# Causal scores of a step in three tiles of probabilities instead of four

## What is computed

```python
q_lat = jnp.einsum('bhsd,hdr->bhsr', q_nope, wuk)
scores = jnp.einsum('bhsr,btr->bhst', q_lat, c_kv) + jnp.einsum('bhsd,btd->bhst', q_rope, k_rope[:, 0])
causal = jnp.tril(jnp.ones((s, s), dtype=bool))
scores = jnp.where(causal, scores, jnp.finfo(scores.dtype).min)
probs = jax.nn.softmax(scores, axis=-1)
out_lat = jnp.einsum('bhst,btr->bhsr', probs, c_kv)
```

## Time and profile before

| | |
|---|---|
| median of 3 runs | 1919.72 us (1919.02 to 1920.83) |
| span of the profiled execution | 1917.3 us |
| instructions | 32648 |
| granted TensorE clock in the attention | 1.00 |

### The profile page before, as it was taken

One profiled execution on the slowest core, in us unless ns is written; L12 is line 12 of the kernel. 1 busy time (PEld: TensorE's weight loads), 2 busy tenths in 40 slices (PEclk: granted clock), 3 DMA queues, 4 the chain that ended last, 5 costly groups with the idle time before them and its releaser, 6 DMA issues.

```text
span 1917.3 us, 32648 instructions
## 1 busy us (share of the span) xinstructions
PE 1909.2 (100%) x10048; PEld 1615.0 (84%) x10048; DVE 1531.8 (80%) x2655; ACT 1168.9 (61%) x2648; POOL 1048.7 (55%) x891
## 2 busy tenths in 40 slices
PE   9999999999999999999999999999999999999999
PEld 7888888888888888888888888888888877888887
DVE  6778888888888887877777777777878889996677
ACT  5456767676758575765555555555656668766441
POOL 5468777787869696865555556555565511000000
PEclk9999999999999999999999999999999999999999
DMA  9838474647474655588546264464628286466645
GB/s 361 333 105 317 133 260 130 253 125 263 122 266 138 231 171 199 195 319 328 181 151 233 77 230 132 158 207 140 217 82 302 91 285 250 198 220 245 229 152 176
DMA packets 86473, 393.13 MB, mean 205 GB/s; under 512 B 9472, under 2 KB 10240, under 8 KB 67328
## 3 DMA queue, kind: packets, MB, share of 16 engines
q1 hardware_dynamic: 86400, 392.21, 58.0%
HBM read 236.46 MB, written 155.71 MB: 205 GB/s over the span
## 4 chain that ended last, share of the span: by engine, by line
PE 97%; DVE 2%; DMA 1%; ACT 0%; issue 0%; DVEq 0%; POOL 0%; ACTq 0%; SPq 0%
PE at_out L1281 11%; PE at_out L1285 10%; PE at_out L1282 10%; PE at_qbank L55 7%; PE at_qbank L57 7%; PE at_qbank L56 7%; PE at_score L1244 6%; PE at_score L1235 3%; PE at_turned L1256 3%; PE at_qbank L1605 3%; PE at_score L1605 2%; PE at_out L1605 2%; PE at_value L56 2%; PE at_value L55 2%; PE at_value L57 2%; PE at_qbank L1608 2%
## 5 line engine op out<-in xcount | busy, mean ns | idle before, releaser
L2620 DVE TENSOR_TENSOR at_acc<-at_out,at_acc 128x512 f32<-128x512 f32 x640 | 438.9, 689 | 138.2 <-PE at_out L1285 136.2
L2266 POOL TENSOR_TENSOR at_acc<-at_stage,at_acc 128x512 f32<-128x512 f32 x256 | 332.3, 1298 | 184.1 <-ACT at_stage L1747 174.5
L1281 PE MATMUL at_out<-at_wvo,at_val_hi 128*128 128x512 f32 x896 | 365.3, 408 | 0.5 <-ACT at_stage L1747 0.2
L1285 PE MATMUL at_out<-at_wvo,at_val_lo 128*128 128x512 f32 x896 | 350.6, 391 | 0.0
L1282 PE MATMUL at_out<-at_wvo,at_val_hi 128*128 128x512 f32 x896 | 350.5, 391 | 0.0
L1747 ACT ACTIVATE at_stage<-at_out 128x512 f32<-128x512 f32 x256 | 153.0, 599 | 125.2 <-PE at_out L1285 112.9
L1787 ACT ACTIVATE at_pT_hi<-at_turned 128x512 fp32r<-128x512 f32 x128 | 76.4, 597 | 245.8 <-PE at_turned L1256 245.8
L2226 POOL TENSOR_TENSOR at_probs<-at_probs,at_row_stats 128x512 f32<-128x512 f32 x128 | 133.3, 1041 | 148.2 <-DVE at_row_stats L2582 148.2
L1781 ACT ACTIVATE at_probs<-at_probs,at_row_stats 128x128 f32<-128x128 f32 x512 | 197.7, 388 | 8.8 <-DVE at_row_stats L2577 8.8
L1285 PEld LDWEIGHTS at_out<-at_wvo,at_val_lo 128*128 128x128 f32 x896 | 168.4, 188 | 37.8
L1281 PEld LDWEIGHTS at_out<-at_wvo,at_val_hi 128*128 128x128 f32 x896 | 169.1, 189 | 31.1 <-DVE at_acc L2620 5.7
(11 more groups left out here) (313 smaller groups left out, 4772.3 us busy)
## 6 DMA issues: line engine op xcount, KB each, us to landing
parts_d<-at_rope_tmp SPq DMA_DIRECT2D x32, 1024.0 KB, 6.1
at_qrope<-parts_d SPq DMA_DIRECT2D x128, 256.0 KB, 5.3
wvo_d<-at_wvo SPq DMA_DIRECT2D x16, 2048.0 KB, 7.8
at_wvo<-wvo_d SPq DMA_DIRECT2D x16, 2048.0 KB, 8.1
ff_w_d<-ff_w SPq DMA_DIRECT2D x21, 1024.0 KB, 6.2
ff_w<-ff_w_d SPq DMA_DIRECT2D x21, 1024.0 KB, 4.8
ab_raw<-in_w_heads SPq DMA_DIRECT2D x32, 576.0 KB, 5.5
wvo_d<-at_wvo SPq DMA_DIRECT2D x16, 1024.0 KB, 9.8
```

The lines of the kernel that those rows point to most:

```text
L1281: pe.matmul(out, hi, weight[:, 0], start=start, stop=False, skip_group_check=True)
L1285: pe.matmul(out, lo, weight[:, 0], start=False, stop=True, skip_group_check=True).then_inc(out_ready, 1)
L2266: pool.tensor_tensor(at, stage[group][z][:], at, ALU.add).then_inc(pool_added, 1)
L2620: dve.tensor_tensor(at, outb[FACTORS[name][2]][:], at, ALU.add).then_inc(added, 1)
```

## The change

The four score tiles of a step become three. Late queries (64 to 127) of both heads of a batch share the rows of one tile with all 128 keys, one tile for each batch. Early queries (0 to 63) of both heads have only keys 0 to 63; both batches stand side by side in the columns of the third tile. For this the queries are stored by half (`half_of`: late or early) with both heads in 128 adjacent columns, so ScalarE writes at_qlat in pieces of 64 and the relayout of the rotated queries writes runs of 64 tokens: 16 DMAs of [32, 8, 64] for four, and the semaphore's counts go from 64 to 256. The turned probabilities are taken out in three pieces on ScalarE and VectorE; their lower left quarter is cleared once, in the opening. The mask covers late keys' half and the early tile. The blocks of values change places, with their homes in memory; the matmuls of values and products keep their sizes.

```diff
@@ relayout_in
                 for j in range(4):
-                    sp.dma_start(as_f32(qrope[c][j * HALF:(j + 1) * HALF]), of[SLOT_OF_PART[j]]).then_inc(
-                        qrope_in[c], 16)
+                    for h in range(QUAD):
+                        to = as_f32(qrope[c][j * HALF:(j + 1) * HALF, h // PAIR, :, h % PAIR])
+                        sp.dma_start(to, of[SLOT_OF_PART[j]][:, h].rearrange("p (k q) -> p k q", q=HQ)).then_inc(
+                            qrope_in[c], 16)
@@ TensorE score_ropes
                 for bl in range(2):
-                    cols = batch_cols(s, bl)
-                    for h in range(PAIR):
-                        pe.matmul(score[:, bl * PAIR + h], qrope[c][:, pair * PAIR + h, cols], rope_keys[:, :, cols],
-                                  start=h == 0, stop=False, skip_group_check=True)
+                    pe.matmul(score[:, bl], both_heads(qrope[c][:, pair, half_of(s, bl, 1)]), rope_keys[:, :, batch_cols(s, bl)],
+                              start=bl == 0, stop=False, skip_group_check=True)
+                for bl in range(2):
+                    pe.matmul(score[:, EARLY, :, early_keys(bl)], both_heads(qrope[c][:, pair, half_of(s, bl, 0)]),
+                              rope_keys[:, :, early_cols(s, bl)], start=bl == 0, stop=False, skip_group_check=True)
@@ TensorE score_rests
                 for bl in range(2):
-                    cols = batch_cols(s, bl)
-                    for h in range(PAIR):
-                        ins = pe.matmul(score[:, bl * PAIR + h, 0], qlat[u % 2][:, h, cols], compressed[c][:, cols],
-                                        start=False, stop=True, skip_group_check=True)
+                    pe.matmul(score[:, bl, 0], both_heads(qlat[u % 2][:, half_of(s, bl, 1)]), compressed[c][:, batch_cols(s, bl)],
+                              start=False, stop=True, skip_group_check=True)
+                for bl in range(2):
+                    ins = pe.matmul(score[:, EARLY, 0, early_keys(bl)], both_heads(qlat[u % 2][:, half_of(s, bl, 0)]),
+                                    compressed[c][:, early_cols(s, bl)], start=False, stop=True, skip_group_check=True)
@@ TensorE turn
-                for j in range(PARTS):
-                    to = TURNED_AT[j]
-                    ins = pe.transpose(turned[:, to * SEQ:(to + 1) * SEQ], probs[s % 2][:, j, :], ident[:])
+                for to, tile in enumerate((1, 0, EARLY)):
+                    ins = pe.transpose(turned[:, to * SEQ:(to + 1) * SEQ], probs[s % 2][:, tile, :], ident[:])
@@ ScalarE
-                act.activation(qlat[u % 2][:, h, :], qbank[use % 2][:], ACT.Copy).then_inc(ql_out, 1)
+                act.activation(qlat[u % 2][:, :, h, :], qbank[use % 2][:].rearrange("p (k q) -> p k q", q=HQ),
+                               ACT.Copy).then_inc(ql_out, 1)
...
-                    ins = act.activation(probs[i][:, j, :], probs[i][:, j, :], ACT.Exp,
-                                         bias=nmax[i][:, j:j + 1], accum_out=sums[i][:, j:j + 1])
+                    rows = probs[i][:, j, :] if j < EARLY else probs[i][:, EARLY, early_keys(j - EARLY)]
+                    ins = act.activation(rows, rows, ACT.Exp, bias=nmax[i][:, j:j + 1], accum_out=sums[i][:, j:j + 1])
...
-                act.activation(pT_hi[:], turned[:], ACT.Copy).then_inc(pT_hi_done, 1)
+                act.activation(pT_hi[:, :, HQ:SEQ], late_turned, ACT.Copy).then_inc(pT_hi_done, 1)
+                for bl in range(2):
+                    act.activation(pT_hi[0:HQ, heads_at(bl), 0:HQ], early_turned[bl], ACT.Copy).then_inc(pT_hi_done, 1)
@@ GpSimd normalise
-                pool.tensor_tensor(probs[i][:], probs[i][:], rsum[i].unsqueeze(2).to_broadcast([P, PARTS, SEQ]),
+                late, early = probs[i][:, LATE], probs[i][:, EARLY].rearrange("p (b k) -> p b k", b=2)
+                pool.tensor_tensor(late, late, rsum[i][:, 0:2].unsqueeze(2).to_broadcast([P, 2, SEQ]), ALU.mult)
+                pool.tensor_tensor(early, early, rsum[i][:, 2:4].unsqueeze(2).to_broadcast([P, 2, HQ]),
                                    ALU.mult).then_inc(probs_ready, 1)
@@ VectorE turn
-                dve.wait_ge(pT_hi_done, STEPS * m + s + 1)
-                dve.tensor_tensor(pT_lo[:], turned[:], as_f32(pT_hi[:]), ALU.subtract).then_inc(pT_lo_done, 1)
+                done = 3 * (STEPS * m + s)
+
+                def early(bl):
+                    to = slice(0, HQ), heads_at(bl), slice(0, HQ)
+                    return dve.tensor_tensor(pT_lo[to], early_turned[bl], as_f32(pT_hi[to]), ALU.subtract)
+
+                dve.wait_ge(pT_hi_done, done + 2)
+                early(0)
+                dve.wait_ge(pT_hi_done, done + 3)
+                dve.tensor_tensor(pT_lo[:, :, HQ:SEQ], late_turned, as_f32(pT_hi[:, :, HQ:SEQ]), ALU.subtract)
+                early(1).then_inc(pT_lo_done, 1)
```

More of the change, by code:

```diff
@@ L136, in decoder, with high @@
     PRODUCTS, PLAIN = 7, 3
[L137 to L142, removed]
+    BLOCKS = PRODUCTS + 1
+    A21, A22, A11, A12, S2, S3, S4, S1 = (slice(j * SEQ, (j + 1) * SEQ) for j in range(BLOCKS))
+    DIRECT, SUMS = slice(SEQ, 4 * SEQ), slice(4 * SEQ, BLOCKS * SEQ)
+    A11_A12, S3_S4 = slice(A11.start, A12.stop), slice(S3.start, S4.stop)
+    HQ, HALVES = SEQ // 2, 2 * BPC
+    LATE, EARLY = slice(0, 2), 2
+    TILES = 3
+    def high(of):
+        return slice(of.start - SEQ, of.stop - SEQ)
     FACTORS = {"P1": (A11, "b11", 0), "P2": (A12, "b21", 1), "P6": (S2, "t2", 0), "P5": (S1, "t1", 0),
@@ L219, in decoder @@
         probs = [home(157696 + 2048 * i, f"at_probs{i}", [P, PARTS, SEQ]) for i in range(2)]
[L220 to L225, removed]
+        pT_both = home(161792, "at_pT", [P, 2, 2 * PAIR, SEQ], F32R)
+        pT_hi, pT_lo = pT_both[:, 0], pT_both[:, 1]
+        val_hi = [home(o, f"at_val_hi{i}", [P, PRODUCTS * SEQ], F32R) for i, o in enumerate((75776, -6144))]
+        val_lo = [home(o, f"at_val_lo{i}", [P, BLOCKS * SEQ], F32R) for i, o in enumerate((79360, 88064))]
+        val_whole = [home(o, f"at_val_whole{i}", [P, BLOCKS * SEQ]) for i, o in enumerate((79360, 88064))]
         stage_at = (4 * (PACK + UNUSED), 4 * UNUSED, 198656)
@@ L316, in decoder @@
         prep_turned = outb[1]
+        late_turned = turned[:, 0:2 * SEQ].rearrange("p (k q) -> p k q", q=HQ)
+        early_turned = [turned[bl * HQ:(bl + 1) * HQ, 2 * SEQ:3 * SEQ].rearrange("p (k q) -> p k q", q=HQ) for bl in range(2)]
         cr_turned, cr_out = qbank, [turned, value]
@@ L396, in batch_cols, with early_cols, half_of, both_heads @@
             return slice(b * SEQ, (b + 1) * SEQ)
+        def early_cols(s, bl):
+            return slice(batch_cols(s, bl).start, batch_cols(s, bl).start + HQ)
+        def half_of(s, bl, late):
+            return 2 * (2 * (s % 2) + bl) + late
+        def both_heads(of):
+            return of.rearrange("p h q -> p (h q)")
+        def early_keys(bl):
+            return slice(bl * HQ, (bl + 1) * HQ)
+        def heads_at(bl):
+            return slice(PAIR, 2 * PAIR) if bl == 0 else slice(0, PAIR)
         def place(s):
@@ L1268, in values @@
                     cols = batch_cols(s, bl)
-                    at = slice(bl * PAIR * SEQ, (bl + 1) * PAIR * SEQ)
-                    ins = three_passes(pe, value[:, at], tok[:, c, KV_HI + cols.start:KV_HI + cols.stop],
+                    at = heads_at(bl)
+                    ins = three_passes(pe, value[:, at.start * SEQ:at.stop * SEQ], tok[:, c, KV_HI + cols.start:KV_HI + cols.stop],
                                        tok[:, c, KV_LO + cols.start:KV_LO + cols.stop],
@@ L1278, in product @@
                 val, op, n = FACTORS[name]
-                out, hi, lo, weight = outb[n][:], val_hi[s % 2][:, val], val_lo[s % 2][:, val], wvo[pair][op]
+                out, hi, lo, weight = outb[n][:], val_hi[s % 2][:, high(val)], val_lo[s % 2][:, val], wvo[pair][op]
                 pe.matmul(out, hi, weight[:, 0], start=start, stop=False, skip_group_check=True)
@@ L2675, in opening @@
                 largest(0, 0)
+                dve.memset(as_f32(pT_both[HQ:P, :, :, 0:HQ]), 0.0)
                 query(N - 1, 1)
@@ L3090, in constants @@
         "ident": np.eye(P, dtype=np.float32),
-        "mask": np.where(np.tril(np.ones((SEQ, SEQ), bool)), 0, MASKED).astype(np.float32),
+        "mask": np.concatenate([np.zeros((P, SEQ // 2)), np.tile(np.where(np.tril(np.ones((SEQ // 2, SEQ // 2), bool)), 0, MASKED),
+                                                                  (2, 1))], axis=1).astype(np.float32),
         "cos": np.tile(cos * root, (QUAD, 1)),
```

42 lines of the change are left out of this document (24 added, 18 removed).

## The result

The changed kernel takes 1945.4 us (median of four runs, 1943.2 to 1947.3), the kernel before 1920.3 on the same chip: a ratio of 1.0129, interval 1.0115 to 1.0144. It is 25 us slower, where 12 us faster was forecast.

The account below looks back on a forecast made before the run. TensorE's matmul stream, 97% of the chain, was taken to bound the kernel: 0.128 us less in each of 128 steps gains 16.4 us, losses 4.4, so 1919.7 - 12.0 gives 1908 us; range 1900 to 1932.

Parts of the forecast that it names:

- What it adds elsewhere: Added work on VectorE, ScalarE and GpSimd, mostly covered; waits in slots 0 and 1, opening and last quad lose 4.4 us.
- The relayout: cost 0, without any cover left: SyncE's 16 issues take 7.6 us for 1.89; raw rope weights queued behind land at 707.9, just not late; cost 0.
- Rival C: Short 256-byte runs make the relayout late, and the raw rope load behind it; 1942 us, or 1925 for half; chance 0.17.
- D: TensorE's f32r matmuls with 128 moving columns are slow, priced as fp32, 0.22 us a step for 0.11; 1936 us; chance 0.06.
- E: Side engines' small strided pieces grow the turn's chain by over 0.66 us, so values wait each step; 1920 us; chance 0.12.
- B: Narrow TensorE matmuls cost what their columns stream, saving another 0.30 us a step; 1874 us; chance 0.10.
- floor: On TensorE a narrower moving operand still costs 0.110 us (f32r, 128 columns) and 0.10 us an fp32 instruction.
- rests: The score block's fp32 matmuls on TensorE: eight instructions before and after, half of them narrow; 0 us gained by the floor.
- the wait for the turn: Slot 0 of group 0's quads: values wait 0.10 to 0.26 us for VectorE's turn, taken as 0.18, in seven quads, 1.3 us.
- opening and last quad: Chains with cover under 0.3 us in three or four slots, and one clearing of turned probabilities; 1.0 us lost.
- the bound of 0.29: VectorE's turn in three pieces for one subtraction grows by at most 0.29 us, taken as 0.21.
- the cover of a plain slot: VectorE's turn ends with 0.66 us to spare before the values' weight load, so its and ScalarE's growth costs nothing there.

Follow-up runs that it names:

- the shifted kernel: The changed kernel with 24 empty VectorE instructions near its start, so its loop over the full quads begins 24 instructions later; 1920.4 us, ratio 1.000 to the kernel before.
- the shift of a loop of the same length: The kernel before with five empty VectorE instructions in each slot of the full loop (297 instructions) and 40 more near the start; 1960.5 us, ratio 1.021.
- the written-out loop: VectorE's six full-quad iterations written out, in the unshifted changed kernel with halves put side by side on the relayout's store: 1906.6 us; in the kernel before: 1920.9 us.
- experiment 5: The changed kernel with 4 empty VectorE instructions near its start; 1956.1 us, ratio 1.019.
- experiment 1: The changed kernel with 24 empty VectorE instructions near its start; 1920.4 us, ratio 1.000 to the kernel before.
- experiment 7: The changed kernel with 24 empty VectorE instructions and the relayout's halves put side by side on the store (256-byte runs), loaded back by 4 DMAs; 1907.4 us, ratio 0.994.
- the cured kernel: The changed kernel with 24 empty VectorE instructions and the relayout's halves put side by side on the store to memory, the kernel of experiment 7; 1907.4 us.

## Why the prediction was wrong

**The step that failed first is one that I did not take**: of the sum over engines, no term asked whether the longer programs still stay on the engines. "What it adds elsewhere" counted VectorE's added instructions by their time, some of them hidden, and never by their number. Forty more in the full loop, placed as they are, cost 4.6 to 6.4 us in slot 0 of five quads, 25.0 us in the end against the shifted kernel. The runs show the cause in three ways: the shift by 24 takes it away, the shift of a loop of the same length brings it into the kernel before, and the written-out loop has none. Not shown is how many stretches stay on VectorE; three, with 257 or 297 instructions, do, and one position more does not. That the boundaries are those of the 8 KB packets is inferred, and the traces bear it out. In the changed kernel a third wait, of 0.4 us, stands ahead of the loop's instruction 136 (five of the six in the row L2668 of the list of waits), 128 instructions behind the second one, and in the quad from 416 us the last two packets of q14 start at 475.89 and 519.93 us, 0.7 and 2.7 us behind the loop's instructions 136 and 264. The Trainium skill, "Vector Engine (DVE) Microarchitecture Reference", section "Instruction fetch and dispatch (NX sequencer)", gives 64 bytes for an instruction, so 128 to a packet, which fits the 128 just seen. With stretches of 128 a loop of 297 that begins one to forty instructions ahead of a boundary touches four of them, and elsewhere three. The changed kernel's begins seven ahead, experiment 5's three ahead, and experiment 1's seventeen behind. A loop of 257 touches three wherever it lies. By this estimate the forty added instructions made the loss possible, in 40 of 128 positions, and its position made it real; the forecast could have counted the first and not the second.

The page of the Trainium skill that would have named it is "Runtime: NRT & Kernel Launch", section "Instruction fetch mechanics": an engine holds a small window of code, fetches ahead only in sequence, and a taken branch whose target is not in the window stalls until it is fetched. With that rule the runs agree: these waits don't occur without a branch back, nor where the loop stays. The section gives blocks of 16 KB and two of them for most engines; the packets of q14 here are 8 KB (0.51 MB in 63), and the 16 KB ones are those of q8 (0.64 MB in 39), so for VectorE the measured size holds.

**"The relayout: cost 0, without any cover left"** is the second step that failed, by 13.0 us (1920.4 to 1907.4). Its arithmetic was near: I had 7.6 us for sixteen issues, they took 8.3. Raw rope weights at most 0.9 us late cost 3.8 us over six quads of the shifted kernel (slot 1 at 14.2 to 15.1 us for 14.0). But I followed only that one load. The rope weights behind the second relayout of the switch quad were issued at 889.05 in the shifted kernel, where they had been at 878.81 before, 4.5 us in the first later quad. The last quad, whose loads for the cross attention stand behind the last relayout, is 4.3 us longer than in experiment 7. The shifted kernel's trace names the load that does the harm there, the tokens for the cross attention: VectorE waits for it, and TensorE for VectorE:

```profile
1470.81 0.69 DVE L2837 BATCH_NORM_STATS2 cr_stats<-cr_x 128x6 f32<-128x512 f32 x1 [2.96 <-DMA cr_x<-x_d]
...
1473.60 0.50 PE L1309 MATMUL at_out<-at_wvo,at_val_hi 128*128 128x512 f32 x1 [3.14 <-DVE at_acc L2668]
```

Experiment 7 has neither wait.

**Rival C had the right time for half a wrong reason.** Its 1942 us lies 3 us from the result, by luck. Its mechanism, small packets that each cost 33 ns or more, did not occur (18 ns, 2.2 us to landing, and experiment 7 has as many of them); its place, loads behind the relayout on SyncE, holds for 13 of the 38 us between the changed and the cured kernel, and the other 25 are code. Cases D and E did not occur. B did in small, and for f32r alone: 0.09 us for 128 columns, where the forecast had 0.110 and B 0.067; the "floor" was a little too high there, for the smallest distance in a trace without narrow matmuls is no floor. The fp32 instructions kept it, 0.81 us for eight. The sustained 81 ns of the section "Back-to-back issue gap" of the Trainium skill's page "TensorE: Matmul & The Clock Gate" was the nearest figure for the 0.09.

**What the forecast said of everything else held in sum, in part by luck.** With both causes removed the kernel takes 1907.4 us where 1908 was forecast. But 128 steps at 0.10 us gain 12.8 us and not 16.4, and as the spans differ by 11.4 (1917.3, 1905.9), 1.4 were lost and not 4.4: two terms too large by about as much. Term by term, from the distances between transposes in that kernel: a step gains 0.10 us, forecast 0.128, though the score block itself is shorter by 0.15 (ropes 0.07, forecast 0.02; transposes 0.08, forecast 0.11; rests 0, as forecast). The other 0.05 us are in matmuls that did not change, some of whose starts stand up to 0.01 us further apart. Over a later quad they come to 0.03 us a step in the latent matmuls, 0.01 in the products and 0.01 in the values; the reason is open. That a plain slot has 9.26 us where 9.27 was forecast is chance: the 9.40 that this started from was 0.04 too much. Slot 0 stays at 10.8 us (its gain is used up by the wait for the turn, forecast 0.18). Slot 1 grows from 13.75 to 14.02 us, 0.27, forecast 0.3 less the gain of 0.13. The opening is as long as before (first transposes at 134.26 us for 134.24), and the last quad is 0.6 us shorter; by the gain of its eight steps that is a loss of 0.2, where opening and last quad were to lose 1.0. VectorE's turn takes 0.95 us from its first start to the next instruction's (334.36 to 335.31; 329.62 to 330.57 in experiment 1) for 0.61: +0.34, above the bound of 0.29, and the cover of a plain slot held as forecast.

The range of 1900 to 1932 would have held the kernel that I had priced, and missed the one that was built.

## What to carry to other kernels

A loop that the profile shows as free of instruction loads is a resource: count the instructions that a change adds to the loop of each engine, and look after it at the instruction queues and at waits "for issue" directly behind a branch back. If they appear, shift the loop by a few empty instructions, shorten it, or write it out. Where one transfer becomes many, follow each transfer that stands behind it on the same queue to its first reader, and put small runs on that side of a trip through memory behind which nothing is due soon.

## What the runs showed of the hardware

- A wait for code at a branch back took 4.1 to 7.2 us, by what was moving beside it, and in most kernels a second one of up to 2.8 us followed a few instructions later. The packet of 8 KB itself took 0.3 to 0.8 us of it. TensorE, made to wait 4.1 us by it, then ran at a granted clock of 0.50 for 5.7 us.
- 24 empty instructions at the start of one engine's program were worth 25 us; 4 of them cost 11 us.
- Weights read at a stride of 8 words took 0.19 to 0.21 us from matmul to matmul, twice those side by side.
- Starts of matmuls with 128-column weights: 0.09 us apart for 128 columns of f32r and 0.115 for 256. Eight fp32 instructions took 0.81 us whether all had 128 columns or half of them 64.
- An issue of a relayout on SyncE took 0.44 to 0.54 us. Packets of 256 bytes took 18 ns each, and sixteen transfers of 64 KB made of them landed as fast as they were issued.
